# First attention of a two-layer kernel: row statistics, roots and large products in a new order on four engines

## The chip, the cores and the metric

One core of a Trainium2 chip runs the whole kernel. Its engines are TensorE (PE), VectorE (DVE), ScalarE (ACT), GpSimd (POOL) and SyncE (SP, which here only issues DMAs); they run side by side and wait for each other by semaphores. The metric is the device time of one launch in microseconds (us). The kernel before takes 1766.92 us, the median of 3 runs (1766.03 to 1767.80).

## The reference

Two layers, each a cross attention and a feed-forward part, work on x, 32 x 64 rows of 512. Only the first attention is in question here:

```
x = x + L0(layernorm(x), ctx)
def L0(text, features):
    features_n = rmsnorm(features, fn_w)              # eps 1e-6
    Q = rmsnorm(text @ Wq.T + bq, qn_w)
    K = rmsnorm(features_n @ Wk.T + bk, kn_w)
    attn = softmax(Q @ K.T / sqrt(512))               # within one batch of 64
    return attn @ features_n
```

Behind it come a sparse feed-forward part (low-rank scores pick one of each 32 hidden units), a second attention with 32 heads, and a gated feed-forward part.

## The kernel before

**Tiles.** The 2048 rows are 16 tiles of 128 (two batches). The first attention (`l0_attention`, lines 179 to 777) is written out tile by tile; each engine has its own program: `sp_steps` (L262), `pool_steps` (L295), `act_steps` (L387), `dve_steps` (L520) and `pe_steps` (L672). Each defines small steps with the tile number as argument and a `body(n)` that calls them; `run` (L250) calls body 0 to body 15, and the last two leave out what belongs to tiles beyond the end. The order in a `body` is the order of work on that engine; nothing else schedules it. Matmuls are in three products of high and low parts (`split_mm`, L66), so most tensors are split into `_hi` (by ACT) and `_lo` (by DVE from PSUM, by POOL from SBUF).

**One pass (body n).** PE projects the keys and the queries of tile n+1 (12 matmuls each), computes the scores of tile n, transposes the normalised rows of tile n+2, multiplies tile n-1's probabilities with the features, transposes the queries and the keys of tile n+1, and ends with the transposition of the probabilities of tile n (L753). That needs the exponential of tile n, so a pass lasts from one L753 to the next.

**Row statistics.** Per tile DVE runs `statistics` (bn_stats L524, bn_aggr L527, two small operations), POOL raises the variance to -1/2 (`roots`, L315 to L323: `rs`, the shift `sh`, and the features' root `crs`), and ACT applies both (`normalise`, L398). All of it is done for tile n+2 in body n, with single buffers.

**Key chain.** DVE adds the bias (`key_bias`, L543), ACT sums the squares (`key_squares`, L421), DVE adds the offset (`key_mean`, L547), POOL takes the root (`key_root`, L336), DVE scales the rows by root and weights (`scale_keys`, L559). The queries have a like chain without the scaling (`query_bias` L551, `query_squares` L427, `query_mean` L555, `query_root` L340), whose root is used in the score step (L584), before the maximum (L586) and the exponential (ACT, L471).

**Large products on POOL.** `features_lo` (L327), `features_T` (L332, low part of the transposed context), `weigh` (L313), and in bodies 7 to 14 `split_w1` (L364), which splits the feed-forward weights that ACT has scaled (L447) and cast (L449). `load_w1` (ACT, L440) of bodies 8 and 10 waits for POOL's split of the piece that it overwrites. Bodies 1 to 4 carry maxima over these weights on DVE (L617), bodies 5 to 8 the statistics of the next stage's first rows (L86), body 9 their root (`pool_rstd`, L102), bodies 10 to 14 their normalisation and transposition.

**The last tile.** In body 14 POOL ends with `split_c1_c2` (L378 to L382), which waits for two casts at the end of ACT's body 14. In body 15 PE runs `filler(pe, 0)` (`low_rank`) before it waits for the exponential, and `filler(pe, 1)` (`hidden(0, 0, 0)`) before the last `attend`. Then comes the feed-forward stage: DVE's `chunk` first computes `low[32:64]` (L979), PE the block scores (L1046), DVE `find_max` (L942).

Of the kernel before, what the change touches and what calls it, by code (L numbers as in the profile page):

```python
# [21 lines left out]
ALU = mybir.AluOpType  # L22
# [148 lines left out]
def l0_attention(nc, ctx, m, prep, fw, a):  # L171
# [5 lines left out]
    def sem(n):  # L177
# [30 lines left out]
    st, mv, ve, rs = sb("ln_st", [P, 6]), sb("ln_mv", [P, 2]), sb("ln_ve", [P, 1]), sb("ln_rs", [P, 1])  # L208
    nm, sh = sb("ln_nm", [P, 1]), sb("ln_sh", [P, 1])
    css, cve, crs4 = sb("css", [P, 1]), sb("cve", [P, 1]), sb("crs", [P, RING])  # L210
    crs = lambda n: crs4[:, n % RING:n % RING + 1]
    kss, kve, krs = sb("kss", [P, 1]), sb("kve", [P, 1]), sb("krs", [P, 1])
    qss, qve, qrs = sb("qss", [P, 1]), sb("qve", [P, 1]), sb("qrs", [P, 1])
# [12 lines left out]
    s_css, s_cve, s_crs, s_cw, s_f, s_fl = (sem("css_ok"), sem("cve_ok"), sem("crs_ok"), sem("cw_ok"), sem("f_ok"),  # L226
                                            sem("f_lo_ok"))
    s_xT, s_xTh, s_xTl, s_cTh, s_cTl = sem("xT_ps"), sem("xT_hi_ok"), sem("xT_ok"), sem("cT_hi_ok"), sem("cT_ok")
    s_q, s_k, s_qb, s_kb = sem("q_ps"), sem("k_ps"), sem("qb_ok"), sem("kb_ok")
    s_kss, s_kve, s_krs, s_kn, s_qss, s_qve, s_qrs = (sem("kss_ok"), sem("kve_ok"), sem("krs_ok"), sem("kn_ok"),  # L230
                                                      sem("qss_ok"), sem("qve_ok"), sem("qrs_ok"))
# [30 lines left out]
    def sp_steps(sp):  # L262
        def load(n):
            sp.wait_ge(cT_in, n * 16)
            if n > 1:
                sp.wait_ge(x_in, (n - 1) * 16)
                sp.wait_ge(c_in_, (n - 1) * 16)
            sp.dma_start(m.x[:, bass.ts(n, D)], x_rows[n]).then_inc(x_in, 16)
            sp.dma_start(craw[:, bass.ts(n % 2, D)], c_rows[n]).then_inc(c_in_, 16)
            sp.dma_start(cT_raw[n % 2][:, :, :], a.l0_ctxT[n]).then_inc(cT_in, 16)  # L270
# [9 lines left out]
        load(1)  # L280
        sp.wait_ge(const_in, 64)
        for n in range(2):
# [6 lines left out]
        for n in range(2, NT):  # L289
# [3 lines left out]
            load(n)  # L293

    def pool_steps(pool):  # L295
# [19 lines left out]
        def roots(n):  # L315
            pool.wait_ge(s_ve, n * 3 + 3)
            pool.tensor_tensor(rs[:, :], ve[:, :], m.neg_half[:, 0:1], ALU.pow).then_inc(s_rs, 1)
            pool.wait_ge(s_rs, n + 1)
            pool.tensor_tensor(sh[:, :], nm[:, :], rs[:, :], ALU.mult).then_inc(s_sh, 1)
            pool.wait_ge(s_cve, n + 1)  # L320
            if n >= RING:
                pool.wait_ge(s_pTl, n - RING + 1)
            pool.tensor_tensor(crs(n), cve[:, :], m.neg_half[:, 0:1], ALU.pow).then_inc(s_crs, 1)  # L323
# [10 lines left out]
        def key_root(n):  # L334
            pool.wait_ge(s_kve, n + 1)
# [6 lines left out]
        def body(n, first=False, ahead=True, project=True):  # L342
            if ahead:
                roots(n + 2)
# [1787 lines left out]
```

## Time and profile before

| | us |
|---|---|
| median of 3 runs | 1766.92 |
| the profiled execution | 1768.54 |
| its span | 1766.8 |
| PE busy over the span | 1643.0 (93%) |
| DVE / ACT / POOL busy | 1214.4 / 738.3 / 538.0 |
| mean granted PE clock | 0.98 |

Busy time is a mean over stages. The first attention lies in the first 215 us of the span, the sparse feed-forward part up to some 590 us, the rest is the second layer. The profile's chain of waits is recorded from 591 us on only, so the first stage is read from windows and timelines. In a timeline a row is start, length, engine, line, operation and shapes; brackets give the idle time of the engine just before, and whose result ended it.

### The profile page before, as it was taken

Reading aid. Unit: us, or ns where it says so; the run is one execution under the profiler, and the core shown is the slowest. Engines: PE = TensorE matmul, PEld = TensorE weight load, DVE = VectorE, ACT = ScalarE, POOL = GpSimd, SP = SyncE. Lnnn points to the kernel's source line nnn. Section 1 sums busy time; section 2 is a strip of 40 time slices with the busy share of each in tenths; the row PEclk is TensorE's granted clock in tenths of the full one; section 3 lists DMA queues with packets and bytes.
Section 4 is the critical chain, followed back from the end, with each engine's and each line's share of the span. In section 5 each row is a group of like instructions: output and inputs, shape, how many; then the busy total and the mean of one; then the engine's idle time right before and its main releaser. Section 6 shows DMA issues by size and latency. Waiting matters only on the chain.

```text
span 1766.8 us, 29139 instructions
## 1 busy us (share of the span) xinstructions
PE 1643.0 (93%) x11036; PEld 1055.1 (60%) x11036; DVE 1214.4 (69%) x2269; ACT 738.3 (42%) x2320; POOL 538.0 (30%) x455
## 2 busy tenths in 40 slices
PE   5888889999999789999999999999999999999887
PEld 4676656666666455665655665665655655665553
DVE  4776686867777688666666666666666666676757
ACT  4457611011111355643643643643643643644640
POOL 5557561212121032223223223223223223223304
PEclk8999999999999899999999999999999999999989
DMA  7233120000000210100100100100100100000002
GB/s 209 105 114 112 62 107 1 1 1 0 0 0 0 84 49 7 60 25 1 37 26 1 36 26 1 36 26 1 36 26 1 36 26 1 7 1 1 1 1 96
DMA packets 19461, 60.12 MB, mean 34 GB/s; under 512 B 4128, under 2 KB 4256, under 8 KB 16528
## 3 DMA queue, kind: packets, MB, share of 16 engines
q1 hardware_dynamic: 17904, 52.13, 8.6%
q10 hardware_dynamic: 1440, 6.29, 1.0%
q8 instruction: 91, 1.49, 0.3%
q14 instruction: 26, 0.21, 0.0%
HBM read 54.22 MB, written 4.19 MB: 33 GB/s over the span
## 4 chain that ended last, share of the span: by engine, by line
PE 51%; DVE 8%; ACT 4%; issue 2%; POOL 1%; DVEq 0%; POOLq 0%; ACTq 0%
PE bank L68 15%; PE bank L70 15%; PE bank L69 15%; PE bank L1894 3%; DVE a_oT_lo L1606 2%; PE bank L1919 1%; ACT a_oT_hi L1382 1%; PE bank L1931 1%; PE bank L1900 1%; DVE wmax L792 1%; DVE x_res L1685 1%; DVE xln L1683 1%; DVE ln_st L86 1%; ACT a_qT_hi L1337 1%; ACT xln L119 0%
## 5 line engine op out<-in xcount | busy, mean ns | idle before, releaser
L1357 ACT ACTIVATE a_prob<-a_prob,a_nmx 128x64 f32<-128x64 f32 x512 | 170.1, 334 | 163.2 <-DVE a_nmx L1590 163.2
L68 PE MATMUL bank<-a_wo_hi,a_oT_hi 128*128 128x512 f16 x512 | 194.3, 379 | 1.7 <-DVE a_oT_lo L1606 1.7
L69 PE MATMUL bank<-a_wo_hi,a_oT_lo 128*128 128x512 f16 x512 | 194.3, 379 | 0.0
L70 PE MATMUL bank<-a_wo_lo,a_oT_hi 128*128 128x512 f16 x512 | 194.2, 379 | 0.0
L68 PE MATMUL bank<-a_big 128*128 128x512 f32 (+1 forms) x416 | 168.3, 405 | 15.4 <-DVE a_big L650 10.3
L1543 DVE SCALAR_TENSOR_TENSOR x_res<-bank,a_oinv,x_res 128x512 f32<-128x512 f32 x128 | 95.8, 749 | 98.7 <-PE bank L70 98.7
L70 PE MATMUL bank<-a_big 128*128 128x512 f32 (+1 forms) x416 | 159.4, 383 | 0.0
L69 PE MATMUL bank<-a_big 128*128 128x512 f32 (+1 forms) x416 | 158.9, 382 | 0.0
L1286 POOL TENSOR_TENSOR a_qrs<-a_qve,neg_half 128x16 f32<-128x16 f32 x32 | 109.4, 3419 | 146.8 <-DVE a_qve L1559 146.8
L909 ACT CAST a_big<-bank 128x512 fp32r<-128x512 f32 x64 | 33.9, 532 | 278.5 <-PE bank L1023 278.5
L68 PE MATMUL bank<-a_xT_hi,a_wq_hi 128*128 128x512 f16 x384 | 145.8, 380 | 1.6 <-DVE a_xT_lo L139 1.0
L69 PE MATMUL bank<-a_xT_hi,a_wq_lo 128*128 128x512 f16 x384 | 145.7, 379 | 0.0
L70 PE MATMUL bank<-a_xT_lo,a_wq_hi 128*128 128x512 f16 x384 | 145.7, 379 | 0.0
L68 PE MATMUL bank<-a_wkv_hi,a_cT_hi 128*128 128x256 f16 x512 | 140.7, 275 | 2.3 <-DVE f_wtop L1623 2.3
L868 POOL TENSOR_TENSOR a_wide<-a_wide 128x448 bf16<-128x448 bf16 x64 | 66.3, 1035 | 244.8 <-DVE a_wide L944 244.8
L70 PE MATMUL bank<-a_wkv_lo,a_cT_hi 128*128 128x256 f16 x512 | 140.5, 274 | 0.0
L69 PE MATMUL bank<-a_wkv_hi,a_cT_lo 128*128 128x256 f16 x512 | 140.4, 274 | 0.0
L1284 POOL TENSOR_TENSOR a_krs<-a_kve,neg_half 128x4 f32<-128x4 f32 x32 | 32.4, 1013 | 331.6 <-DVE a_kve L1568 331.6
L1273 POOL TENSOR_TENSOR a_prob<-a_prob,a_mask 128x512 f32<-128x512 f32 x64 | 79.8, 1267 | 140.3 <-DVE a_prob L1584 140.3
L1547 DVE SCALAR_TENSOR_TENSOR a_qT_lo<-bank,a_qT_hi 128x512 f16<-128x512 f32 x128 | 88.2, 691 | 45.5 <-ACT a_q L1338 45.5
L1606 DVE SCALAR_TENSOR_TENSOR a_oT_lo<-bank,a_oT_hi 128x512 f16<-128x512 f32 x128 | 82.0, 683 | 37.3 <-ACT a_oT_hi L1382 37.3
L1278 POOL TENSOR_TENSOR a_prob<-a_prob,a_rden 128x512 f32<-128x512 f32 x64 | 68.6, 1074 | 118.9 <-DVE a_rden L1595 118.9
(308 smaller groups left out, 4209.7 us busy)
## 6 DMA issues: line engine op xcount, KB each, us to landing
shared<-in_l_wq SPq DMA_DIRECT2D x8, 1024.0 KB, 4.9
shared<-in_l_wo SPq DMA_DIRECT2D x8, 1024.0 KB, 4.9
shared<-in_w ACTq DMA_DIRECT2D x6, 896.0 KB, 5.0
a_wide<-in_l_ctxT SPq DMA_DIRECT2D x16, 256.0 KB, 3.7
shared<-in_l_wkv SPq DMA_DIRECT2D x8, 512.0 KB, 3.5
out_x<-x_res SPq DMA_DIRECT2D x16, 256.0 KB, 2.0
x_res<-in_x SPq DMA_DIRECT2D x15, 256.0 KB, 2.7
shared<-in_ctx SPq DMA_DIRECT2D x15, 256.0 KB, 3.8
```

Of the source, the lines that this page charges most:

```text
L68: pe.matmul(out, a_hi, b_hi, start=first, stop=False)
L69: pe.matmul(out, a_lo, b_hi, start=False, stop=False)
L70: return pe.matmul(out, a_hi, b_lo, start=False, stop=last)
L868: pool.tensor_tensor(rank[q % 2][:, :].rearrange("p (b s) -> p b s", s=SPARSE), eq[q % 2][:, :].rearrange("p (b s) -> p b s", s=SPARSE), d ...
L1273: pool.tensor_tensor(blocks(prob[u][:, :]), blocks(prob[u][:, :]), mask[:, :].unsqueeze(1).broadcast_to([P, NB, S]), ALU.add).then_inc(s_m ...
L1278: pool.tensor_tensor(blocks(prob[u][:, :]), blocks(prob[u][:, :]), rden[:, u * NB:(u + 1) * NB].unsqueeze(2).broadcast_to([P, NB, S]), ALU ...
L1286: pool.tensor_tensor(qrs[:, :], qve[:, :], m.neg_half[:, :], ALU.pow).then_inc(s_qrs, 1)
L1357: ins = act.activation(pt, pt, ACT.Exp, bias=nmx[:, col:col + 1], accum_out=den[:, col:col + 1])
L1543: dve.scalar_tensor_tensor(xt, o_banks[t % 2][:, :], oinv[:, c:c + 1], xt, ALU.mult, ALU.add).then_inc(s_x, 1)
L1547: dve.scalar_tensor_tensor(part(qT_lo, j), blocks(q_banks[j][:, :]), SUM_DOWN, part(qT_hi, j), ALU.mult, ALU.subtract).then_inc(s_ql, 1)
L1606: ins = dve.scalar_tensor_tensor(oT_lo[half], blocks(pv_banks[u][b][:, :]), OUT_DOWN, oT_hi[half], ALU.mult, ALU.subtract)
L1894: ins = pe.transpose(sq_banks[t][:, b * P:(b + 1) * P], q2[:, b // 2, 2 * t + b % 2, :], m.ident[:, :])
```

## The change

- SP: the loads of rows and of context are two steps. `load_x` runs one tile further ahead than `load_c`, and in `load_c` the transposed context comes before the plain one.
- Row statistics: `statistics(n + 3)` instead of `(n + 2)` in body n, with mean and variance, root and shift in two buffers each, and without DVE's small operations.
- Roots: the offset (and the factor) is applied by POOL in a `tensor_scalar` of its own before each power; DVE's `features_mean`, `key_mean`, `query_mean` go. The new `root` has two instructions and a semaphore between them.
- Order on DVE: `key_bias(n + 1)`, `statistics(n + 3)`, `scale_keys(n + 1)`, `query_bias(n + 1)`, then the scores.
- Order on ACT: `features(n + 2)` and `features_T(n + 2)` before `key_squares(n + 1)`; `scale_w1` (the first half of the old `split_w1`) behind `key_squares`; `query_squares(n + 1)` behind the last use of the probabilities' high part.
- Order on POOL: `query_root(n)`, `features_root(n + 2)`, `row_root(n + 3)`, (body 9: `pool_rstd`), `key_root(n + 1)`, a wait for `scale_keys(n + 1)`, and only then the large products. The query root of a tile moves from the end of the body before to the front of its own.
- Into the next stage: DVE computes `low[32:64]` before the last `attended`; PE issues the first two block scores before the last `attend`.

```diff
     def sp_steps(sp):
...
-        load(1)
+        load_c(1)
+        load_x(1)
         sp.wait_ge(const_in, 64)
+        load_x(2)
...
-            load(n)
+            load_c(n)
+            if n + 1 < NT:
+                load_x(n + 1)
     def pool_steps(pool):
...
+        def root(out, mean, down, eps, done):
+            pool.tensor_scalar(out, mean, down, eps, ALU.mult, ALU.add).then_inc(s_rve, 1)
+            pool.wait_ge(s_rve, next(roots))
+            pool.tensor_tensor(out, out, m.neg_half[:, 0:1], ALU.pow).then_inc(done, 1)
+
+        def row_root(n):
+            pool.wait_ge(s_ve, n * 2 + 2)
+            if n >= 2:
+                pool.wait_ge(s_xn, n - 1)
+            root(rs(n), mv2[:, n % 2, 1:2], 1.0, LN_EPS, s_rs)
             pool.wait_ge(s_rs, n + 1)
+            pool.tensor_scalar(sh(n), mv2[:, n % 2, 0:1], -1.0, rs(n), ALU.mult, ALU.mult).then_inc(s_sh, 1)
...
         def body(n, first=False, ahead=True, project=True):
+            query_root(n)
             if ahead:
-                roots(n + 2)
+                features_root(n + 2)
+            if n + 3 < NT:
+                row_root(n + 3)
+            if n == ROOT_AT:
+                prep.pool_rstd(pool, 0)
             if project:
                 key_root(n + 1)
+                pool.wait_ge(s_kn, n + 2)
             if ahead:
+                features_T(n + 2)
                 features_lo(n + 2)
-                features_T(n + 2)
-            if project:
-                query_root(n + 1)
             if n < NT - 3:
                 weigh(n + 3)
-            if n == ROOT_AT:
-                prep.pool_rstd(pool, 0)
             if n - 1 in SPLIT_AT:
                 split_w1(SPLIT_AT[n - 1])
             if project and not ahead:
                 split_c1_c2()
     def act_steps(act):
...
                 normalise(n + 2)
...
-            if project:
-                key_squares(n + 1)
             if ahead:
                 features(n + 2)
                 features_T(n + 2)
             if project:
-                query_squares(n + 1)
+                key_squares(n + 1)
+            if n in SPLIT_AT:
+                scale_w1(SPLIT_AT[n])
             act.wait_ge(s_nmx, n * 2 + 2)
...
             act.activation(pT_hi[:, :], b_pT, ACT.Copy, scale=crs(n)).then_inc(s_pTh, 1)
+            if project:
+                query_squares(n + 1)
     def dve_steps(dve, before_last):
...
         def body(n, first=False, ahead=True, project=True):
-            if ahead:
-                statistics(n + 2)
-                features_mean(n + 2)
             if project:
                 key_bias(n + 1)
-                key_mean(n + 1)
+            if n + 3 < NT:
+                statistics(n + 3)
+            if project:
+                scale_keys(n + 1)
                 query_bias(n + 1)
-                scale_keys(n + 1)
...
-        run(body, attended)(dve)
+        run(body)(dve)
+        before_last()
+        attended(NT - 1)
...
-            l0.dve(dve)
+            l0.dve(dve, lambda: low_lo(0, first_low))
...
+                    pe.wait_ge(l0.cl_ok, 2)
+                    pe.wait_ge(l0.s_qb, NT)
+                    pe.wait_ge(l0.s_kb, NT)
+                    block_scores(0, 0, 0, 0, False, True)
+                    block_scores(0, 0, 0, 1, False, True)
```

The prologue before body 0 is put into the like order: on POOL `features_T(0)`, `row_root(0)`, `features_root(0)`, `weigh(0)`, `key_root(0)`, `row_root(1)`, `features_T(1)`, `features_lo(0)`, `features_root(1)`, `weigh(1)`, `row_root(2)`, `features_lo(1)`, `weigh(2)`.

## Rows read from the trace of the kernel before

**Rows 1.** Windows: busy us (instructions) of PE, PEld, DVE, ACT, POOL; PE clock, DMA share, GB/s.
```profile
60.00:75.00 15.00, 12.53 (x61) 9.64 (x59) 11.92 (x23) 7.67 (x21) 8.52 (x11) 0.89 0.32 115
...
400.00:500.00 100.00, 98.99 (x511) 69.01 (x509) 74.60 (x133) 12.01 (x23) 20.18 (x21) 1.00 0.00 0
```

**Rows 2.** Timeline, PE: the transposition of the probabilities that ends a tile's pass.
```profile
51.38 0.27 PE L753 MATMUL bank<-ident,a_prob 128*128 128x128 f32 x1
...
89.02 0.33 PE L753 MATMUL bank<-ident,a_prob 128*128 128x128 f32 x1 [0.46 <-ACT a_prob L471]
...
137.36 0.33 PE L753 MATMUL bank<-ident,a_prob 128*128 128x128 f32 x1 [0.46 <-ACT a_prob L471]
...
149.41 0.48 PE L753 MATMUL bank<-ident,a_prob 128*128 128x128 f32 x1 [0.45 <-ACT a_prob L471]
...
160.25 0.33 PE L753 MATMUL bank<-ident,a_prob 128*128 128x128 f32 x1 [0.15 <-ACT a_prob L471]
...
173.37 0.33 PE L753 MATMUL bank<-ident,a_prob 128*128 128x128 f32 x1
...
204.84 0.27 PE L753 MATMUL bank<-ident,a_prob 128*128 128x128 f32 x1
```

**Rows 3.** Timeline, DVE: pass of tile 8, and the last tile's key scaling.
```profile
130.07 0.68 DVE L524 BATCH_NORM_STATS2 a_ln_st<-x_res 128x6 f32<-128x512 f32 x1
...
131.20 0.74 DVE L543 SCALAR_TENSOR_TENSOR a_wide<-bank,a_crs,shared 128x512 f32<-128x512 f32 x1
133.63 0.15 DVE L547 TENSOR_SCALAR a_kve<-a_kss 128x1 f32<-128x1 f32 x1 [1.68 <-ACT shared L421]
...
134.44 1.75 DVE L559 SCALAR_TENSOR_TENSOR a_wide<-a_wide,a_krs,shared 128x512 f32<-128x512 f32 x1
136.12 0.34 DVE L584 SCALAR_TENSOR_TENSOR a_prob<-bank,a_qrs,a_off 128x128 f32<-128x128 f32 x1
...
202.57 0.75 DVE L559 SCALAR_TENSOR_TENSOR a_wide<-a_wide,a_krs,shared 128x512 f32<-128x512 f32 x1
```

**Rows 4.** Timeline, ACT: the same pass.
```profile
128.74 0.94 ACT L449 CAST w_hi<-shared 128x896 f16<-128x896 f32 x1
...
132.16 0.81 ACT L398 ACTIVATE a_wide<-x_res,a_ln_sh,a_ln_rs 128x512 f32<-128x512 f32 x1 [1.86 <-POOL a_ln_sh L319]
132.89 0.61 ACT L421 ACTIVATE shared<-a_wide 128x512 f32<-128x512 f32 x1
...
134.01 0.61 ACT L414 CAST a_big<-a_wide 128x512 fp32r<-128x512 f32 x1
```

**Rows 5.** Timeline, POOL: one early product, then the same pass.
```profile
4.73 1.26 POOL L332 TENSOR_TENSOR a_big<-a_wide,a_big 128x512 fp32r<-128x512 f32 x1 [1.32 <-ACT a_big L414]
...
131.30 0.56 POOL L317 TENSOR_TENSOR a_ln_rs<-a_ln_ve,neg_half 128x1 f32<-128x1 f32 x1 [1.57 <-DVE a_ln_ve L530]
131.94 0.19 POOL L319 TENSOR_TENSOR a_ln_sh<-a_ln_nm,a_ln_rs 128x1 f32<-128x1 f32 x1
...
134.38 1.27 POOL L327 TENSOR_TENSOR a_big<-a_wide,a_big 128x512 fp32r<-128x512 f32 x1
135.60 1.72 POOL L332 TENSOR_TENSOR a_big<-a_wide,a_big 128x512 fp32r<-128x512 f32 x1
...
137.79 1.30 POOL L313 TENSOR_TENSOR a_wide<-shared 128x512 f32<-128x512 f32 x1
139.05 1.91 POOL L364 TENSOR_TENSOR w_lo<-shared,w_hi 128x896 f16<-128x896 f32 x1
```

**Rows 6.** Groups by line, POOL, whole span.
```profile
L102 POOL TENSOR_TENSOR ln_rs<-ln_ve,neg_half 128x4 f32<-128x4 f32 x12 | 12.1, 1012 | 123.4 <-DVE ln_ve L97 123.4
```

**Rows 7.** Timeline, DVE and POOL: from the last tile's scores into the second stage.
```profile
208.20 0.35 DVE L584 SCALAR_TENSOR_TENSOR a_prob<-bank,a_qrs,a_off 128x128 f32<-128x128 f32 x1 [1.11 <-PE bank L70]
...
209.20 3.97 POOL L382 TENSOR_TENSOR c2st<-h,c2st 32x1792 fp32r<-32x1792 f32 x1
...
217.24 0.63 DVE L942 TENSOR_REDUCE a_wide<-bank 128x14 f32<-128x448 f32 x1 [0.63 <-PE bank L1046]
```

More of the change, by code:

```diff
@@ L313, in weigh, with features_root @@
             pool.tensor_tensor(cw[:, :], craw[:, bass.ts(n % 2, D)], fnw, ALU.mult).then_inc(s_cw, 1)
[L315 to L317 removed]
+        roots = iter(range(1, 4 * NT + 1))
+        def root(out, mean, down, eps, done):
[7 more added lines that the diff above has]
+            root(rs(n), mv2[:, n % 2, 1:2], 1.0, LN_EPS, s_rs)
             pool.wait_ge(s_rs, n + 1)
[L319 to L320 removed]
+            pool.tensor_scalar(sh(n), mv2[:, n % 2, 0:1], -1.0, rs(n), ALU.mult, ALU.mult).then_inc(s_sh, 1)
+        def features_root(n):
+            pool.wait_ge(s_css, n + 1)
             if n >= RING:
                 pool.wait_ge(s_pTl, n - RING + 1)
[L323 removed]
+            root(crs(n), css[:, :], 1.0 / D, L0_EPS, s_crs)
         def features_lo(n):
@@ L366, in pool_steps @@
         features_T(0)
-        roots(0)
+        row_root(0)
+        features_root(0)
         weigh(0)
+        key_root(0)
+        row_root(1)
         features_T(1)
-        key_root(0)
-        roots(1)
-        query_root(0)
         features_lo(0)
+        features_root(1)
         weigh(1)
+        row_root(2)
         features_lo(1)
@@ L397, in normalise @@
             act.wait_ge(s_sh, n + 1)
-            act.activation(xn[:, :], m.x[:, bass.ts(n, D)], ACT.Identity, bias=sh[:, :], scale=rs[:, :]).then_inc(s_xn, 1)
+            if n:
+                act.wait_ge(s_xT, n)
+            act.activation(xn[:, :], m.x[:, bass.ts(n, D)], ACT.Identity, bias=sh(n), scale=rs(n)).then_inc(s_xn, 1)
         def features(n):
@@ L440, in load_w1, with scale_w1 @@
             act.dma_start(w1_raw[p % 2], a.w1[:, p * W1P:(p + 1) * W1P]).then_inc(w1_in[p % 2], 16)
-        def split_w1(s):
+        def scale_w1(s):
             p = s // 2
@@ L510, in act_steps @@
         key_squares(0)
+        normalise(1)
         squares_c(1)
-        normalise(1)
-        query_squares(0)
         rows_T(1)
@@ L977, in chunk @@
                     dve.wait_ge(l0.cl_ok, 2)
-                dve.wait_ge(s_lowh, c + 1)
-                dve.scalar_tensor_tensor(low[32:64, :], (first_low if first else low_bank)[32:64, :], LOW_DOWN, low[32:64, :], ALU.mult,
-                                         ALU.subtract).then_inc(s_lowl, 1)
+                else:
+                    low_lo(c, low_bank)
                 for t in range(TPC):
@@ L1076, in chunk @@
                             if what == "i":
-                                block_scores(c, t, n, q, before, first)
+                                if not (first and t == 0 and q < 2):
+                                    block_scores(c, t, n, q, before, first)
                             elif not (first and t == 0 and q == 0):
```

89 lines of the change are left out of this document (43 added, 46 removed).

## The prediction, written before the changed kernel ran

> **What bounds the kernel now.** I read the windows first: in the second stage PE is busy for 98.99 of 100 us, in the first attention for 12.53 of 15 [rows 1]. So only the first stage has waits to give back, and since PE is full behind it, what it gives back moves the end one for one. The chain of waits does not reach this stage, so I then took each engine's timeline of one pass. The passes are long: 37.64 us for passes 2 to 4 (12.55 each), 48.34 for 5 to 8 (12.08), 12.05 for 9, 10.84 for 10, 13.12 for 11, 31.47 for 12 to 14 (10.5) [rows 2]. PE waits at the end of most for the exponential (0.45 us), which is the end of one chain through all four engines: key bias at 131.20, its squares on ACT at 132.89, offset 133.63, root, key scaling at 134.44, scores at 136.12 [rows 3, 4]. Two delays in it are plain. ACT idles 1.86 us before `normalise`, waiting for POOL's shift, whose power waited 1.57 us for statistics that DVE began only at 130.07, ahead of the key bias [rows 3 to 5]; the key squares stand behind it on ACT, and DVE idles 1.68 us for them. And `scale_keys` takes 1.75 us where POOL runs `features_lo` and `features_T` beside it, 0.75 where it doesn't [rows 3].
>
> **The change part by part.** "Step" is the distance from one start to the next on an engine.
>
> *The large products behind the key rows.* `scale_keys` steps 1.68 us now (134.44 to 136.12); alone I take 0.66: its 0.75 less the overlap that the same rows show. That is -1.02 on the chain in each of passes 1 to 13; the last one had it already. `features_T` gets shorter too, 1.72 to 1.26 [rows 5]. The products must still be ready for PE's next pass: `features_T` ends 1.3 us after the scaling, PE starts 1.7 us or more after it (query bias 0.62, scores, maximum, exponential): hidden, by 0.3 us or so. Beside them now run DVE operations with one operand in PSUM; the row of such a product (`weigh`, 1.30) lies beside two of these and is no longer than one alone, so I take 0, the other end being the 1.0 just named. `features_lo` kept its 1.27 us while `scale_keys` waited. The Trainium skill's page "SBUF — State Buffer", section "SBUF: two separate sides", says that GpSimd and a VectorE operation with two SBUF inputs exclude each other for the whole instruction; by that rule the first 1.2 us of the 1.75 are a wait, and the rows agree with it.
>
> *Query bias behind the scaling:* it filled the time in which DVE waited for the key root, now it steps 0.62 on the chain (an estimate from its neighbours, near the 0.66 above): +0.62 a pass.
>
> *Statistics a tile earlier.* Passes 2 to 8 have extra DVE work at the front (maxima, the next stage's statistics), so the key bias is late there. `statistics` and the small means, 131.20 - 130.07 = 1.13 us, go from in front of it [rows 3]: -1.13. But POOL's new order has `row_root(n + 3)` ahead of `key_root(n + 1)`, and it waits for exactly these statistics, which now follow the key bias. From the key bias's start: 0.68 to the statistics, 0.91 for them, then `row_root`: offset 0.19, hand-over 0.08, power 0.55, hand-over 0.08, shift 0.14, and `key_root`: 0.19, 0.08, 0.55, with 0.08 and 0.03 for the hand-overs between engines, together 3.56 us to the scaling against 134.44 - 131.20 = 3.24 now: +0.32. In passes 2 to 8 the sum is -1.02 + 0.62 - 1.13 + 0.32 = -1.21; where ACT and not DVE is late (7, 8) the same comes out another way (`scale_w1` leaves for 1.09, `query_squares` comes for 0.61; the cast-to-squares stretch of 4.86 us becomes 3.94 with the idle gone and the two feature casts of 0.5 in it; POOL's row root takes 0.5 back; -0.48 - 0.92 + 0.6 - 1.02 + 0.62 = -1.2). Seven passes: -8.5.
>
> *The roots' offsets on POOL.* The trace has no `tensor_scalar` there. The nearest row is the two-input product on one element of `ln_sh`, 0.19 us; the far end is the power, 0.56 [rows 5]; below, the offset can't go under DVE's 0.15 by much, since that row replaces it [rows 3]. I take 0.19, already in the sums. Four or five a pass, three on the chain. The skill's "GPSIMD Engine Reference", section "3.1 Elementwise — side-by-side cycle accounting", gives GpSimd two software dispatch hops an instruction where VectorE has one; that speaks against moving tiny operations there, and 0.19 against 0.15 is what the rows show of it.
>
> *Passes 9 and 11* have ACT wait for POOL's split of a weight piece (1.91 [rows 5]), which ends 0.3 us later in the pass than now since all products start behind the keys. Behind it ACT now has, before the key squares, cast, context squares, `normalise` and both feature casts. Pass 9 has `pool_rstd` (1.01 [rows 6], with its shift 1.25) in front of `key_root` as well, where it was behind everything: worked through, 12.45 us, +0.4. Pass 11: 12.6, -0.5. *Pass 10* has neither: POOL's queue (three products and a split, then four roots of 0.82 and a shift) ends its key root at 7.4 us of the pass, and 2.5 us later comes the end: 9.9, -0.95. *Passes 12 to 14* carry the next stage's rows on ACT and four transpositions more on PE; q, k and these must follow the query bias, which is now later: -0.33, -0.33, +0.1. *Pass 1* is at PE's own length in a slow-clock stretch: 0. *The prologue:* the second tile's rows reach PE some 1.8 us earlier, but POOL has weigh, low parts and roots of three tiles before body 0's key root, so I give it -1.0 (between +1 and -2).
>
> *Loads.* SP issues the context of a tile when its `features_T` two tiles back is done, now some 1.5 us later in the pass; it is needed one pass and a half after, the rows of x later still: 0, if the pass stays above 9 us.
>
> *The last tile.* This is where the change loses. `query_root(15)` ran in body 14; now it opens POOL's body 15, and POOL's body 14 ends with `split_c1_c2`, whose second product takes 3.97 us and ended at 213.17, while the last scores started at 208.20 [rows 7]. In the new order scores 15 need that root. Counted from the transposition of tile 14 (204.84): the product ended at 8.33, now at 9.25 since ACT has `query_squares(15)` in front of the two casts that it needs; root 0.9; scores at 10.2 instead of 3.36; maximum, exponential, transposition at 11.35 instead of 7.03, because `low_rank` (12 matmuls) hid part before: +4.3. Then the hidden matmuls, the two block scores (0.45) and `attend`; the block scores and `low` no longer stand between the last rows and `find_max`: -0.85. The first `find_max`, at 12.40 before [rows 7], comes at 15.85: +3.45.
>
> Sum: -8.5 + 0.4 - 0.95 - 0.5 - 0.66 + 0.1 - 1.0 + 3.45 = -7.7 us. PE's clock takes some of it back. The granted clock is 0.89 in a window of this stage and 1.00 in the next [rows 1]; 0.11 x 15 us x 2 is a stretch of 3.3 us at the lower level of 1.2 GHz. It fell into pass 3 [rows 2], which like its neighbours has slack, and cost nothing there; in a shorter pass it costs up to 1 us, and after the new idle stretch of 3.3 us before tile 15's transposition the hidden matmuls (2.1 us) may run at 1.2 GHz for another 2. I put 1.7 for both. That leaves -6. The profiled execution took 1768.54 us, 1.74 more than its span and 1.62 above the median; the same difference applied to the median gives **1761 us**.
>
> **Rivals.**
> - *The offsets on POOL are dear* (the slower side). Three lie on the chain in each of passes 1 to 13, four where POOL's queue is the bound. Each 0.1 us above 0.19 costs 4.3 us in all; from 0.19 + 7.7/43 = 0.37 us on the change gains nothing, and at the power's 0.56 it costs 16: 1766.9 - 7.7 + 16 = 1775. For it: powers of one element take 0.55. Against: the product of one element takes 0.19.
> - *The clock takes all.* The new idle stretch and two or three slow stretches in passes that now have no slack: -7.7 + 2.3 + 3 x 1.2 = -1.8: 1765. For it: idle time in the passes does not go away but shrinks. Against: the slow stretch in pass 3 left its length unchanged.
> - *The products' lock moves instead of going.* If `weigh`, low parts and split block the DVE operations that now stand beside them (query bias, scores, attended rows), about 1 us a pass returns and with the last tile's +3.45 the time is 1766.9 - 6 + 13 = 1774. Against it stand the PSUM rows above.
> - *More is gained*: POOL takes `row_root` before the key squares are done wherever ACT is late (10 to 14), the prologue gives its 2 us, the clock costs nothing: 1766.9 - 11 = 1756.
> - *The change doesn't do what it says:* the statistics are ahead, yet their root stands before the key root; that is priced at 0.3 to 0.5 a pass and in the forecast.
>
> **How the numbers follow.** Forecast 0.48 (its own range 1758 to 1764), more gained 0.17, clock 0.17, dear offsets 0.12, moved lock 0.06. The range 1753 to 1772 leaves out the far ends of the two slow cases and little below. Faster by over 0.2% (3.5 us, about what a measurement tells from no change): nearly all of the first, all of the second, some of the third: 0.62; within 0.2%: 0.2; slower: 0.18.
>
> **What would show it.** `scale_keys` at 0.75 us in every pass; passes 2 to 8 near 11.3, 11, 10; POOL's `tensor_scalar` at 0.2; `row_root` between the statistics and the key root; scores of the last tile behind a 4 us product on POOL, and the first `find_max` some 15.9 us after tile 14's transposition. Wrong would be: key scaling still above 1.5, offsets above 0.35, or the last scores early.

## The result and the profile after

The changed kernel takes 1771.08 us (median of 15 runs, 1769.43 to 1774.04), the kernel before beside it 1767.78 (15 runs, 1765.55 to 1769.30): ratio 1.0020, 95% interval 1.0012 to 1.0028. It is slower, by 0.2%; forecast were 1761 (between 1753 and 1772) and faster. The profiled execution took 1770.39 us with a span of 1768.6 and a mean granted clock of 0.976.

The windows, with the columns of [rows 1]; the first query is of the kernel after, its first window the prologue:

```profile
21.00:31.00 10.00, 7.07 (x21) 5.31 (x20) 1.52 (x3) 1.43 (x3) 3.40 (x6) 0.66 1.11 271
60.00:75.00 15.00, 12.88 (x62) 10.39 (x61) 11.61 (x19) 8.26 (x20) 7.61 (x15) 0.89 0.32 116
...
400.00:500.00 100.00, 98.99 (x511) 68.94 (x509) 75.47 (x134) 11.70 (x23) 20.88 (x21) 1.00 0.00 0
```

The second stage is as full as it was, so the question stays in the first 215 us. PE's timeline, transposition of the probabilities (L772 is L753 of before), answers to [rows 2]:

```profile
46.73 0.42 PE L772 MATMUL bank<-ident,a_prob 128*128 128x128 f32 x1
...
90.95 0.33 PE L772 MATMUL bank<-ident,a_prob 128*128 128x128 f32 x1
...
135.15 0.33 PE L772 MATMUL bank<-ident,a_prob 128*128 128x128 f32 x1
148.63 0.42 PE L772 MATMUL bank<-ident,a_prob 128*128 128x128 f32 x1
...
172.32 0.42 PE L772 MATMUL bank<-ident,a_prob 128*128 128x128 f32 x1
...
202.43 0.27 PE L772 MATMUL bank<-ident,a_prob 128*128 128x128 f32 x1
213.71 0.33 PE L772 MATMUL bank<-ident,a_prob 128*128 128x128 f32 x1 [2.91 <-ACT a_prob L505]
```

Passes 2 to 4 are 11.46 us each (12.55), pass 8 (124.71 to 135.15) 10.44 (11.24). But pass 0 ends at 46.73, where it ended at 41.45, and the last pass is 11.28 us instead of 7.03. Laid side by side, what moved `find_max` from 217.24 to 218.24 us:

| part | forecast | measured |
|---|---|---|
| prologue and pass 0 | -1.0 | +5.28 |
| pass 1 | 0 | -0.08 |
| passes 2 to 8 | -8.5 | -7.41 |
| pass 9 | +0.4 | +1.43 |
| pass 10 | -0.95 | -0.72 |
| pass 11 | -0.5 | +0.45 |
| passes 12 to 14 | -0.56 | -1.36 |
| last pass | +4.3 | +4.25 |
| to `find_max` | -0.85 | -0.84 |
| clock | +1.7 | (inside the above) |
| sum | -6 | +1.0 |

Behind `find_max` the span is another 0.8 us longer (1550.36 against 1549.56).

**A pass.** DVE and POOL in pass 8 of the kernel after, the pass of [rows 3, 5]:

```profile
128.67 0.73 DVE L574 SCALAR_TENSOR_TENSOR a_wide<-bank,a_crs,shared 128x512 f32<-128x512 f32 x1
129.32 0.68 DVE L561 BATCH_NORM_STATS2 a_ln_st<-x_res 128x6 f32<-128x512 f32 x1
...
132.64 0.75 DVE L582 SCALAR_TENSOR_TENSOR a_wide<-a_wide,a_krs,shared 128x512 f32<-128x512 f32 x1 [2.42 <-POOL a_krs L326]
133.31 0.68 DVE L578 TENSOR_TENSOR a_wide<-bank,shared 128x512 f32<-128x512 f32 x1
```

```profile
126.92 1.92 POOL L387 TENSOR_TENSOR w_lo<-shared,w_hi 128x896 f16<-128x896 f32 x1
128.81 0.19 POOL L324 TENSOR_SCALAR a_qrs<-a_qss 128x1 f32<-128x1 f32 x1
129.08 0.55 POOL L326 TENSOR_TENSOR a_qrs<-a_qrs,neg_half 128x1 f32<-128x1 f32 x1
...
130.63 0.19 POOL L324 TENSOR_SCALAR a_ln_rs<-a_ln_mv 128x1 f32<-128x1 f32 x1
...
131.78 0.19 POOL L324 TENSOR_SCALAR a_krs<-a_kss 128x1 f32<-128x1 f32 x1
132.06 0.55 POOL L326 TENSOR_TENSOR a_krs<-a_krs,neg_half 128x1 f32<-128x1 f32 x1
133.47 1.28 POOL L349 TENSOR_TENSOR a_big<-a_wide,a_big 128x512 fp32r<-128x512 f32 x1 [0.87 <-DVE a_wide L582]
```

The key scaling is 0.75 us, as in all 16 tiles. The offsets cost 0.19. The idle time sits elsewhere now: DVE waits 2.42 us for the key root, and POOL is not waiting for anything before it. It goes from the split (L387) straight through the query root, the features' root, the row root and the shift to the key root, 3.8 us without a gap. The chain of this pass runs through POOL's list of small operations.

**The prologue.** POOL and PE; PE's block of 12 matmuls is the projection of tile 1's keys:

```profile
20.61 0.60 POOL L324 TENSOR_SCALAR a_krs<-a_kss 128x1 f32<-128x1 f32 x1 [4.90 <-ACT shared L451]
...
22.21 0.95 POOL L326 TENSOR_TENSOR a_ln_rs<-a_ln_rs,neg_half 128x1 f32<-128x1 f32 x1
...
23.48 1.27 POOL L349 TENSOR_TENSOR a_big<-a_wide,a_big 128x512 fp32r<-128x512 f32 x1
```

```profile
24.90 0.76 PE L68 MATMUL bank<-a_big 128*128 128x512 f32 x1 [2.93 <-POOL a_big L349]
...
29.73 0.63 PE L70 MATMUL bank<-a_big 128*128 128x512 f32 x1
30.15 1.01 PE L695 MATMUL bank<-ident,a_wide 128*128 128x128 f32 x4
```

`features_T(1)` (L349) now stands behind the root of tile 0's keys and tile 1's row root. PE waits 2.93 us for it and starts the projection at 24.90 instead of 22.90. Then the 12 matmuls start 0.43 us apart (0.56 behind the first), where before they started 0.23 apart (0.33): the granted clock is 0.50 from 24.90 to 30.15, all of it the lower level of 1.2 GHz, and was 0.98 from 22.90 to 27.40 before. `rows_T(1)` (L695) follows at 30.15. Its counterpart came at 27.43:

```profile
22.90 0.49 PE L68 MATMUL bank<-a_big 128*128 128x512 f32 x1
...
25.27 0.39 PE L69 MATMUL bank<-a_big 128*128 128x512 f32 x1
25.50 0.39 PE L70 MATMUL bank<-a_big 128*128 128x512 f32 x1
27.43 0.66 PE L676 MATMUL bank<-ident,a_wide 128*128 128x128 f32 x4 [1.54 <-ACT a_wide L398]
```

**The last tile.** POOL, then DVE and PE, of the kernel after; compare [rows 7]:

```profile
207.49 3.95 POOL L407 TENSOR_TENSOR c2st<-h,c2st 32x1792 fp32r<-32x1792 f32 x1
211.53 0.19 POOL L324 TENSOR_SCALAR a_qrs<-a_qss 128x1 f32<-128x1 f32 x1
211.80 0.55 POOL L326 TENSOR_TENSOR a_qrs<-a_qrs,neg_half 128x1 f32<-128x1 f32 x1
```

```profile
212.45 0.35 DVE L606 SCALAR_TENSOR_TENSOR a_prob<-bank,a_qrs,a_off 128x128 f32<-128x128 f32 x1 [7.30 <-POOL a_qrs L326]
...
218.24 0.62 DVE L961 TENSOR_REDUCE a_wide<-bank 128x14 f32<-128x448 f32 x1
```

The scores wait 7.30 us for a root that stands behind the product of 3.95 us.

### The profile page after: what moved, and what is told of

Its sections match the earlier page's. It is cut to its first block, busy times and chain, and to the rows that moved or that the text cites. A ratio compares the mean times of both kernels' runs of the same rounds, so it can differ in the third digit from the quotient of the medians.

```text
span 1768.6 us, 29226 instructions
## 1 busy us (share of the span) xinstructions
PE 1644.5 (93%) x11036; PEld 1058.4 (60%) x11036; DVE 1191.4 (67%) x2173; ACT 737.5 (42%) x2320; POOL 547.8 (31%) x519
## 4 chain that ended last, share of the span: by engine, by line
PE 51%; DVE 8%; ACT 4%; issue 2%; POOL 1%; DVEq 0%; POOLq 0%; ACTq 0%
PE bank L68 15%; PE bank L69 15%; PE bank L70 15%; PE bank L1920 3%; DVE a_oT_lo L1632 2%; PE bank L1945 1%; ACT a_oT_hi L1408 1%; PE bank L1957 1%; PE bank L1926 1%; DVE wmax L811 1%; DVE x_res L1711 1%; DVE xln L1709 1%; DVE ln_st L86 1%; ACT a_qT_hi L1363 1%; ACT xln L119 0%
```

## The experiments

Twelve kernels, each timed in five rounds against the kernel before. "Passes 1 to 14" is the stretch between the ends of pass 0 and pass 14 in the profiled run. The ratios are to the kernel before on the same chip (medians 1767.59 to 1768.03). The times of pass 0 and `find_max` are counted from the start of the profiled execution, and they hold the wait for the first loads: PE's first matmul starts at 9.5 to 11.0 us in all kernels but e4, where it starts at 12.79.

| kernel | median us | ratio (95%) | end of pass 0 | passes 1 to 14 | last pass | find_max |
|---|---|---|---|---|---|---|
| before | 1767.8 | 1 | 41.45 | 163.39 | 7.03 | 217.24 |
| after | 1771.08 | 1.0020 (1.0012, 1.0028) | 46.73 | 155.70 | 11.28 | 218.24 |
| e1 | 1765.82 | 0.9989 (0.9980, 0.9998) | 41.82 | 155.93 | 11.23 | 213.51 |
| e2 | 1766.61 | 0.9996 (0.9987, 1.0005) | 46.21 | 155.72 | 7.71 | 214.10 |
| e3 | 1765.68 | 0.9992 (0.9983, 1.0001) | 44.03 | 151.63 | 11.06 | 211.25 |
| e4 | 1765.95 | 0.9994 (0.9985, 1.0003) | 48.30 | 151.09 | 11.24 | 216.83 |
| e5 | 1752.10 | 0.9910 (0.9895, 0.9924) | 38.77 | 147.05 | 8.34 | 198.63 |
| e6 | 1787.28 | 1.0114 (1.0099, 1.0129) | 47.92 | 169.70 | 11.27 | 235.11 |
| e7 | 1754.49 | 0.9933 (0.9920, 0.9946) | 38.51 | 151.72 | 8.24 | 202.94 |
| e8 | 1751.66 | 0.9907 (0.9892, 0.9921) | 39.86 | 147.53 | 8.16 | 200.02 |
| e9 | 1769.43 | 1.0010 (1.0001, 1.0019) | 42.68 | 156.32 | 11.26 | 214.81 |
| e10 | 1763.51 | 0.9978 (0.9969, 0.9987) | 39.72 | 158.86 | 8.20 | 212.16 |
| e11 | 1759.86 | 0.9955 (0.9941, 0.9969) | 41.19 | 155.96 | 6.90 | 209.42 |
| e12 | 1747.34 | 0.9883 (0.9868, 0.9898) | 38.60 | 142.75 | 10.01 | 196.00 |

**e1: `features_T(1)` first in POOL's prologue.**

```diff
         weigh(0)
+        features_T(1)
         key_root(0)
         row_root(1)
-        features_T(1)
```

> The changed kernel with one edit in POOL's prologue: features_T(1) stands before key_root(0) and row_root(1) again. My theory: the first pass of the changed kernel ends 5.3 us late (L772 at 46.73 against L753 at 41.45) because project_k(1) waits for features_T(1), which ends at 24.75, and then runs all its 12 matmuls at the lower clock. With the edit they start at 22.9 and step at 0.25 us: the first rows_T(1) moves from 30.15 to about 26, the first pass ends at about 42.5, the whole is 4 us shorter, ratio to the kernel before 0.9995. Rival (the order of the loads on SP or POOL's long queue of 13 steps sets the first pass, not this wait): the first pass still ends above 45.5 and the time moves by less than 1.2 us.

Pass 0 ends at 41.82 us, the passes behind it keep their length, and the median is 5.3 us below the changed kernel's. `rows_T(1)` comes at 25.66, 1.77 ahead of the kernel before, as the prediction had it for the whole change. PE starts tile 1's projection at 22.76, at the higher level from the second matmul on:

```profile
22.76 0.56 PE L68 MATMUL bank<-a_big 128*128 128x512 f32 x1
23.16 0.39 PE L69 MATMUL bank<-a_big 128*128 128x512 f32 x1
```

One line of order in the prologue costs more than the whole result. The two intervals (0.9998 against 1.0012) don't meet.

**e9: only the row root behind it.** `key_root(0)`, `features_T(1)`, `row_root(1)`.

> The changed kernel with features_T(1) between key_root(0) and row_root(1) in GpSimd's prologue, so that only the key root (0.60 + 0.55 us) still stands in front of it. Theory A (PE's projection waits for features_T(1), and the price grows with the lateness): features_T(1) ends at about 23.1 us, the projection starts at some 23.3 us instead of 24.9 (22.9 in the kernel before, 22.8 with features_T(1) in front of both), at the higher clock from its second or third matmul on; pass 0 starts at 42 to 43 us instead of 46.7, find_max at 213.5 to 215 us, ratio 0.999 to 1.000. Theory B (any pause before this projection costs the higher clock for all 12 matmuls): the projection takes 5.2 us as in the changed kernel, rows_T(1) comes at 28.5 us, and pass 0 starts at 44.5 to 45.5 us.

PE waits 1.18 us, starts at 23.70 and keeps the higher level; pass 0 ends at 42.68. In the profile this undoes 4.0 of the 5.3 us, in the medians only 1.65 (1.0010, with an interval that overlaps the changed kernel's). The place is settled; what this half of the move is worth in time isn't. (Here `features_T(1)` starts beside tile 0's key scaling, which takes 1.63 us instead of 0.75; that was not followed up.)

```profile
23.70 0.47 PE L68 MATMUL bank<-a_big 128*128 128x512 f32 x1 [1.18 <-POOL a_big L349]
```

**e2: the last query root ahead of `split_c1_c2`.**

```diff
-            query_root(n)
+            if n < NT - 1:
+                query_root(n)
...
             if project and not ahead:
+                query_root(n + 1)
                 split_c1_c2()
```

> The changed kernel with query_root(15) moved from the front of POOL's body 15 to body 14 ahead of split_c1_c2. My theory: the last scores wait for nothing but this root behind a product of 3.95 us; the last pass goes from 11.28 back to 7.0 us, the time falls by 4.3 us less what low_rank still hides, ratio 0.9995. Rival (the idle stretch is only covered another way, since the following stage is bound by POOL's split_w2): the last pass shortens, but the end moves by under 1.5 us.

The last pass is 7.71 us, so 3.57 of its 4.25 us come back; `find_max` is 4.1 us earlier, the median 4.5 us. The cause was right, and its size nearly.

**e3: query bias ahead of the key scaling.** DVE's order as it was before. (It needs a wait of the bias for the squares of the tile before, which are later on ACT now.)

```diff
             if project:
-                scale_keys(n + 1)
                 query_bias(n + 1)
+                scale_keys(n + 1)
```

> The changed kernel with query_bias before scale_keys on DVE again (with a wait for the query squares of the tile before, which are long done). DVE idles 2.1 us before scale_keys for the key root, so the bias of 0.62 us fits there. My theory: 0.62 us a pass, and in passes 5, 9 and 11, where q and k transposes ran at the lower clock behind the bias, up to 1 us more: in all 9 to 11 us, ratio 0.9965. Rival (POOL's order alone sets the passes; PE's queries then wait for project_q): less than 4 us.

Passes 2 to 8 are 3.76 us shorter, 0.54 a pass, where the prediction charged 0.62; pass 1 gives back 1.1 and pass 0 gains 2.7. In time -5.4 us, about half of what was expected: DVE waits 2.4 us for the key root, and the 0.68 us of the bias fit into that.

Not all of pass 0's gain is the edit's. The edit changes nothing ahead of tile 1's projection, and PE starts that block as late as in the changed kernel (24.94, behind 2.87 us), but only its first half runs at the lower level. `rows_T(1)` comes 1.04 us earlier than in the changed kernel, and `features_lo(0)` and body 0's key root on POOL 1.45 us earlier:

```profile
24.94 0.77 PE L68 MATMUL bank<-a_big 128*128 128x512 f32 x1 [2.87 <-POOL a_big L349]
...
29.11 0.60 PE L697 MATMUL bank<-ident,a_wide 128*128 128x128 f32 x4
```

**e4: key root ahead of the row root (and of `pool_rstd`).**

```diff
+            if project:
+                key_root(n + 1)
             if n + 3 < NT:
                 row_root(n + 3)
             if n == ROOT_AT:
                 prep.pool_rstd(pool, 0)
             if project:
-                key_root(n + 1)
                 pool.wait_ge(s_kn, n + 2)
```

> The changed kernel with POOL's key_root(n+1) ahead of row_root(n+3) and pool_rstd. My theory: in passes 2 to 6 key_root starts when the key squares end instead of 1.3 us later (after statistics and row_root), in 7 and 8 0.6 earlier, in pass 9 2.2 earlier: 5 x 1.2 + 1.1 + 2.2 + about 1 elsewhere = 10 us less, ratio 0.996. Rival (row_root now stands before features_T, so project_k of the next pass waits for its low part): features_T ends after L772 and most of the gain goes, under 3 us.

Passes 2 to 8 are 7.58 us shorter (1.08 each, about the 1.15 that row root and shift take from 130.63 to 131.78). Then pass 10 gives 3.3 back. `find_max` reads only 1.4 us earlier than in the changed kernel, but the first matmul of this execution is 2.6 us late, so 4.0 is the fair figure; the median is 5.1 us lower, half of the 10 expected and more than the rival's 3. `features_T` stands behind the row root and `pool_rstd`, PE waits for it, and the matmuls behind the wait run at the lower level:

```profile
141.43 1.03 POOL L102 TENSOR_TENSOR ln_rs<-ln_ve,neg_half 128x4 f32<-128x4 f32 x1
...
142.69 1.27 POOL L349 TENSOR_TENSOR a_big<-a_wide,a_big 128x512 fp32r<-128x512 f32 x1
```

```profile
144.01 0.80 PE L68 MATMUL bank<-a_big 128*128 128x512 f32 x1 [1.50 <-POOL a_big L349]
```

It is the prologue's fault again, at another place: a projection's last input behind small roots. There are two prices more. The row root's offset now starts beside the key scaling in 13 tiles, and takes as long as the scaling, 0.75 us, instead of 0.19:

```profile
126.83 0.75 DVE L583 SCALAR_TENSOR_TENSOR a_wide<-a_wide,a_krs,shared 128x512 f32<-128x512 f32 x1 [2.11 <-POOL a_krs L326]
```

```profile
126.87 0.75 POOL L324 TENSOR_SCALAR a_ln_rs<-a_ln_mv 128x1 f32<-128x1 f32 x1
```

And behind the idle stretch of 3.39 us at the end, nine of the 12 hidden matmuls start 0.37 us apart (0.19 in the changed kernel, behind 2.91), so `find_max` comes 6.20 us after the last transposition and not 4.53. The same is seen in e6 (3.39 us, 6.22).

**e6: no wait for the scaled keys.**

```diff
                 key_root(n + 1)
-                pool.wait_ge(s_kn, n + 2)
```

> The changed kernel with one wait less: GpSimd goes from the key root straight to features_T, features_lo and weigh, without waiting for the scaled keys. Theory A (the 1.75 us of the key scaling before was sharing with a large GpSimd product beside it): scale_keys goes back from 0.75 us to about 1.75 in nearly every pass, the passes 1 to 14 grow by 0.8 to 1.1 us each, some 13 us in all, and the ratio to the kernel before is about 1.009 (it is 1.002 for the changed kernel). Theory B (the scaling was slow for the scalar operand or for its place in the order, not for the neighbour): scale_keys stays at 0.75, the products start 0.8 us earlier, and the time stays or falls a little.

Theory A: +14.0 us in passes 1 to 14 (13 expected), +16.2 us in time, ratio 1.0114 (1.009 expected). Beside `features_T` the scaling takes 1.74 to 1.77 us in tiles 1 to 14, and the product behind it 1.72 instead of 1.27:

```profile
68.81 1.74 DVE L581 SCALAR_TENSOR_TENSOR a_wide<-a_wide,a_krs,shared 128x512 f32<-128x512 f32 x1 [2.10 <-POOL a_krs L326]
```

```profile
68.74 1.26 POOL L349 TENSOR_TENSOR a_big<-a_wide,a_big 128x512 fp32r<-128x512 f32 x1
69.96 1.72 POOL L344 TENSOR_TENSOR a_big<-a_wide,a_big 128x512 fp32r<-128x512 f32 x1
```

The last tile has a longer product beside it, and the scaling grows by the same 0.64 us, to 2.38: it ends some 0.55 us behind the product either way.

```profile
213.15 1.90 POOL L386 TENSOR_TENSOR w_lo<-shared,w_hi 128x896 f16<-128x896 f32 x1
```

```profile
213.22 2.38 DVE L581 SCALAR_TENSOR_TENSOR a_wide<-a_wide,a_krs,shared 128x512 f32<-128x512 f32 x1 [1.70 <-POOL a_krs L326]
```

**e10: the wait alone, in the kernel before.**

```diff
             if project:
                 key_root(n + 1)
+                pool.wait_ge(s_kn, n + 2)
```

> The kernel before with one line more: behind key_root(n+1) GpSimd waits for the scaled keys before it goes on to features_lo, features_T and the query root. Nothing else of the change is in it. Theory A (the key scaling shares with the large product, and its 1.0 us lies on the path of every pass): scale_keys takes 0.75 us instead of 1.75, passes 1 to 14 are 0.6 to 1.0 us shorter each, find_max at 204 to 209 us instead of 217.2, ratio 0.992 to 0.995: the wait alone gains more than the whole change. Theory B (GpSimd's products are then late themselves: features_lo for ScalarE, and the query root behind them for the scores): scale_keys at 0.75 us, but the scores start later by what the keys gained, find_max within 3 us of 217, ratio 0.998 to 1.002.

Between the two. The scaling is 0.75 us in all tiles. Passes 2 to 8 are 7.4 us shorter, 1.05 each, as in the changed kernel (78.60 and 78.57 us; 85.98 before). But pass 1 is 2.3 us longer (behind a pass 0 that ends 1.7 earlier) and pass 10 1.0, so that passes 1 to 14 together are only 4.5 us shorter; the last pass is 1.2 longer. In all 14, PE now waits 0.6 to 1.1 us for `features_T`, which is second behind `features_lo`:

```profile
128.46 0.75 DVE L560 SCALAR_TENSOR_TENSOR a_wide<-a_wide,a_krs,shared 128x512 f32<-128x512 f32 x1
```

```profile
129.29 1.28 POOL L327 TENSOR_TENSOR a_big<-a_wide,a_big 128x512 fp32r<-128x512 f32 x1 [0.87 <-DVE a_wide L560]
130.52 1.27 POOL L332 TENSOR_TENSOR a_big<-a_wide,a_big 128x512 fp32r<-128x512 f32 x1
```

```profile
131.85 0.50 PE L68 MATMUL bank<-a_big 128*128 128x512 f32 x1 [1.07 <-POOL a_big L332]
```

**e11: the wait, and `features_T` ahead of `features_lo`.**

```diff
             if ahead:
-                features_lo(n + 2)
                 features_T(n + 2)
+                features_lo(n + 2)
```

> The kernel before with the wait for the scaled keys behind key_root(n+1), as in the last run, and features_T ahead of features_lo. With the wait alone find_max came at 212.2 us (217.2 before), with passes of 9.8 to 13.0 us: in the pass of tile 8 PE paused 1.07 us in front of its projection for features_T, which stood behind features_lo, and in the next ones it waited for the rows. Theory A (the wait pushes features_T onto the path, since it stands second): no such pause, passes 1 to 14 shorter by 0.3 to 0.5 us each than with the wait alone, find_max at 206 to 209 us, ratio 0.993 to 0.996. Theory B (features_lo and the query root behind it are as urgent): find_max within 2 us of 212.2, ratio 0.997 to 0.999.

Passes 1 to 14 take 155.96 us, as in the changed kernel (155.70), with nothing else of the change in it. `find_max` comes at 209.42, a little outside theory A's window; the ratio, 0.9955, is inside. PE's wait for `features_T` is gone, yet passes 2 to 8 are no shorter than in e10 (78.47 and 78.60 us), and in five of the seven PE waits for the normalised rows of tile n+2 instead (1.79 us in pass 5). What this edit gains lies at the ends: passes 0 and 1 together 0.3, passes 12 to 14 1.4, the last pass 1.3; passes 9 to 11 lose 0.4. Why the last passes gain was not followed up.

**e7, e5, e8, e12: the edits together.** e7 is e1, e2 and e3; e5 adds e4; e8 is e5 with `features_T` ahead of the row root and `pool_rstd`; e12 is e8 with the weight split ahead of `features_lo` and `weigh`:

```diff
             if project:
                 key_root(n + 1)
                 pool.wait_ge(s_kn, n + 2)
             if ahead:
                 features_T(n + 2)
             if n + 3 < NT:
                 row_root(n + 3)
             if n == ROOT_AT:
                 prep.pool_rstd(pool, 0)
+            if n - 1 in SPLIT_AT:
+                split_w1(SPLIT_AT[n - 1])
             if ahead:
                 features_lo(n + 2)
             if n < NT - 3:
                 weigh(n + 3)
-            if n - 1 in SPLIT_AT:
-                split_w1(SPLIT_AT[n - 1])
```

> The changed kernel with three edits at once: features_T(1) ahead of key_root(0) and row_root(1) in GpSimd's prologue, the last tile's query root ahead of split_c1_c2, and query_bias ahead of scale_keys on VectorE. Alone each took find_max from 218.2 us to 213.5, 214.1 and 211.3 us. Theory A (the three places are apart: prologue, last tile, the passes between): they add up, except that the third gained 2.7 of its 7 us in the prologue, where the first now stands; find_max at 204 to 207 us and a time of 1757 to 1762 us, ratio 0.994 to 0.997. Theory B (the time in front of find_max is given back behind it by a lower clock): find_max early, but the rest behind it longer than 1553 us, and a time of 1763 to 1766 us.

> The three edits and the fourth: key_root ahead of row_root and pool_rstd on GpSimd. Alone the fourth made passes 2 to 9 some 9.9 us shorter and passes 10 and 11 some 3.7 longer, as PE waited there for features_T behind row_root and pool_rstd. Theory A: on top of the three it gains 0.3 to 1 us in passes 2 to 9, and loses in pass 10 what PE waits for features_T; find_max 2 to 6 us ahead of the kernel with three edits, ratio 0.992 to 0.995. Theory B (query_bias in front already hides row_root, since key_root waits for the squares on ScalarE anyway): no gain over three edits, and the pause before the projection in pass 10 makes it the slower of the two.

> As the kernel with four edits, but row_root(n+3) and pool_rstd stand behind features_T instead of in front of it: key_root, wait for the scaled keys, features_T, row_root, pool_rstd, features_lo, weigh. Theory A (features_T is what the projection waits for, as in pass 10): pass 10 comes without the pause of 1.5 us and its low clock, some 10.3 us instead of 13.4, and find_max 2 to 5 us ahead of the kernel with four edits. Theory B (row_root is then too late for ScalarE's normalise of the next pass, or features_lo 1 us later for ScalarE): the passes grow by some tenths each and the two are equal.

> As the kernel with four edits and features_T ahead of row_root (find_max at 200.0 us, passes 9 to 11 of 13.2, 11.7 and 13.9 us), with GpSimd's split_w1 ahead of features_lo and weigh. There ScalarE idled 4.15 us in pass 11 until GpSimd's split of a piece was done, so that the normalised rows came 2.2 us late for PE, and the transpositions and the next projection ran at the lower clock. Theory A (the split is what holds ScalarE): it comes 2.6 us earlier in bodies 7 to 14, ScalarE's pause falls to about 1.5 us, passes 9 and 11 are 1 to 2 us shorter each, find_max at 196 to 198 us, ratio 0.988 to 0.990. Theory B (features_lo and weigh 1.9 us later hold ScalarE's features of the next pass instead): passes 8 to 14 equal or longer, ratio 0.990 to 0.992.

The three add up, to more than theory A expected: e7 is 16.6 us below the changed kernel. e5 gains another 2.4 over it in the medians (the two intervals just touch) and 4.3 at `find_max`, with pass 10 at 12.66 us (10.45 in e7) for the reason of e4. e8, expected 2 to 5 us ahead at `find_max` or equal, equals e5 (0.9907 and 0.9910): passes 2 to 8 are as short, and pass 10 is 11.7, but passes 9 and 11 are longer (13.2 and 13.9 against 12.6 and 12.1). There ACT waits for the split of a weight piece, the rows come late, and PE transposes them at the lower level:

```profile
149.73 0.94 ACT L486 CAST w_hi<-shared 128x896 f16<-128x896 f32 x1 [4.15 <-POOL w_lo L390]
```

```profile
152.75 1.11 PE L700 MATMUL bank<-ident,a_wide 128*128 128x128 f32 x4 [2.18 <-ACT a_wide L430]
```

e12 shortens the wait to about 1.45 us, passes 9 and 11 to 10.7 and 11.2, and takes 4.3 us off: 1747.34 us, 1.2% below the kernel before. It beats both kernels. Its last pass is 10.0 us where e8 has 8.2; that was not followed up.

```profile
143.29 0.94 ACT L486 CAST w_hi<-shared 128x896 f16<-128x896 f32 x1 [1.45 <-POOL w_lo L390]
```

## Why the prediction was wrong

**The step that failed** is the prologue, "-1.0 (between +1 and -2)" with "the second tile's rows reach PE some 1.8 us earlier". It was +5.28, outside its own bounds of +1 and -2, and it turned a gain into no gain. PE takes its work in order, and `rows_T(1)` stands behind the projection of tile 1's keys. The prediction followed the rows and not what is in front of them: the projection needs `features_T(1)`, which the diff moves behind 2.9 us of small operations (20.61 to 23.48). From the traces the 5.28 divides so: `features_lo(0)` on POOL starts at 32.38 instead of 29.30 (+3.08; the projection starts 2.0 late and takes 2.4 longer at the lower level, and part of that was slack before); from there to body 0's key root POOL now has six roots with their offsets where three powers stood, 10.60 us instead of 8.64 (+1.96); from that root to the scores -0.41, as the scaling is short; from the scores to the end of the pass +0.65, with PE's key transposition at 1.06 us. e1 shows that the first of these is the lever: with it undone, `features_lo(0)` starts at 27.48, and pass 0 ends within 0.4 us of before. It also shows the second fault of the term. The rows do come 1.77 us early in e1, but POOL's longer row of small roots (+1.95) takes all of it, so even with the rows early the term is +0.4 and not -1.0. That the projection's clock carries a part, and not its lateness alone, e3 bears out by chance: the same late start with half the slow matmuls brings body 0's key root 1.45 us earlier.

With this term at its measured size the forecast would have been 1767, no change. None of the prediction's signs of being wrong (key scaling above 1.5, offsets above 0.35, last scores early) came about; none of them looked at the prologue. The prologue makes 6.3 us of the 10 between forecast and result. The passes fell short by 2.4, of which the 1.7 put aside for the clock covered most; the rest is the 2.3 us by which the medians moved more than `find_max`, and a median of the kernel before that was 0.9 higher in 15 runs than in three.

**The passes:** -7.69 where -10.1 was forecast before the clock's share. (The 1.7 for the clock was meant for one of these passes and for the hidden matmuls behind tile 15; those ran at the higher level, 0.19 us apart, though in e4 and e6 they didn't.) The single prices were near. Key bias to key scaling was put at 3.56 us and takes 3.65 (61.87 to 65.52 in pass 2) and 3.97 in pass 8. The key scaling steps 0.67 to the next operation (0.66). The query bias costs 0.54 (0.62), by e3. The row root in front costs more than the +0.32 of the forecast once the squares come early: 1.08 a pass, by e4. Passes 9 and 11 are a microsecond each above forecast. In pass 9 PE idles 3.52 us before the query transposition and then runs it and the key transposition at the lower level:

```profile
146.93 1.05 PE L719 MATMUL bank<-ident,a_wide 128*128 128x128 f32 x4 [3.52 <-DVE a_wide L578]
147.78 1.06 PE L725 MATMUL bank<-ident,a_wide 128*128 128x128 f32 x4
```

A transposition takes 0.43 us to the next start at the higher level and 0.85 here, so pass 9 loses 0.8 to it, and passes 5 and 11, where the key transposition alone takes 1.02 and 0.90 us, up to half as much each. That is the rival "the clock takes all" in part: by this estimate 1.5 us or so in all. It decided nothing alone.

**The last tile** was right in place and size: forecast 11.35 us for the last pass and +3.45 at `find_max`, measured 11.28 and +3.41. e2 takes most of it away again.

**The rivals.** "The offsets on POOL are dear": 0.19 us each, it fell, though in pass 8 the row of roots is the bound by its number. Only where an offset starts beside the key scaling (e4, e5) does it cost 0.75. "More is gained" fell with the prologue. "The lock moves": it fell; the DVE operations beside the products keep their length (0.68 for the query bias, 0.34 for the scores). e6 and e10 bear out the lock itself from both sides, 1.75 against 0.75 by a single wait. The Trainium skill's "SBUF — State Buffer", section "SBUF: two separate sides", has GpSimd and a VectorE operation with two SBUF inputs exclude each other for the whole instruction; these rows agree, and so do the 2.38 us of e6 and the 0.75 us of the offset in e4; the query bias and the scores, with an operand in PSUM, stayed free.

**What e10 and e11 say of the change.** In passes 2 to 8 the whole gain can be had with one line, the wait behind the key root (78.60 against 78.57 us), and in passes 1 to 14 with that and `features_T` in front (155.96 against 155.70). The statistics a tile earlier, four roots in one row, the query bias behind the scaling and the rest of the new order together added nothing to it, and that order cost 5.3 us at the start and 3.4 at the end.

**Still open:** medians and profiles don't agree to the microsecond. In the changed kernel and the ten built on it the time (by the ratios) stands some 2 us higher, on average, against before's than `find_max` does (-0.7 to +4.6); in e10 and e11 by +1.2 and -0.1. The lowest of these is e4 with its late start; counted from the first matmul it is +1.9. So the prediction's premise that what this stage gives back moves the end one for one held only to within 2 us or so. The 20 us behind `find_max` have a granted clock of 0.77 in the kernel after and 0.85 before, but e11 and e12 share 0.83 with unlike remainders, so the clock there isn't shown to be the cause.

## What to carry to other kernels

When an order of work is rewritten, price its two ends as carefully as its steady pass: here the steady part gained 7.7 us and prologue and last tile lost 8.7. For every small operation that moves in front of a large one, ask which block of matmuls takes the large one's result; 2 us of lateness there cost over twice that (4.9 us at the end of pass 0, by e1), in part since the block behind it ran at the lower clock. And try the one wait that removes the contention by itself, with the urgent product first behind it, before moving anything else.

## What the runs showed of the hardware

- In these rows GpSimd and VectorE hold each other up where VectorE's operation has two inputs in SBUF. The key scaling takes 0.75 us alone, 1.74 to 1.77 beside a product of 1.27 and 2.38 beside one of 1.90 (e6). The other way round, a `tensor_scalar` on one element that starts 0.05 us after the scaling takes 0.75 us instead of 0.19 (e4; in two tiles of e5 it kept its 0.19, and the power behind it took 0.86). An operation with one operand in PSUM is not held up (0.68 for the query bias, 0.34 for the scores).
- The long small operations of POOL at the start are the same thing, and not a price of their first use: in the kernel after, offsets take 0.60 us at 9.51 and again at 20.61, powers 0.95 at 10.19 and again at 22.21, a shift 0.84 at 11.25, each begun while such an operation of VectorE runs (9.34 to 12.05, 20.51 to 21.17, 22.00 to 22.75). Between them, at 13.63 and 13.91, an offset takes 0.19 and a power 0.57.
- The granted clock after a pause of PE: behind 2.93 us all 12 matmuls of the block at the lower level (steps of 0.43 us), but behind 2.87 us at the same place in e3 only six; behind 1.50 us (e4) twelve; behind 1.14 us in e10 none in pass 5 and seven in pass 10; behind 1.18 us (e9) none but at most the first. So the length of the pause alone does not tell which level follows. In e8 four transpositions behind 2.18 us took 1.11 us, in e3 those behind 2.54 us took 0.66.
